# Value bias added on VectorE in the values' bank, epsilon added to one column, and no bias row on TensorE: a fused transformer layer

## The reference

```
ln(x)  = (x - mean) / sqrt(var + 1e-5)
x  = x + attn(ln(x));   x = x + ffn(ln(x))
attn(x): n = ln(x)*w + b;  Q, K = elu(n @ qk_w + qk_b) + 1   (64 features)
         V = n @ v_w + v_b                                  (256 features)
         out_t = sum_{s<=t} (q_t.k_s) V_s / (sum_{s<=t} q_t.k_s + 1e-6)
         x = x + out @ o_w + o_b;  x = x + gelu((ln(x)*w + b) @ f1 + f1_b) @ f2 + f2_b
ffn(x):  h = gelu(x @ ternary(W_fc));  (ln(h)*w + b) @ ternary(W_proj)
```

## Time and profile before

| | us |
|---|---|
| median of 3 runs (467.3 to 470.79) | 467.65 |
| the profiled execution's own time | 467.8 |
| its span, in which all rows below lie | 465.8 |
| PE, DVE, ACT busy in the span | 448.6, 369.0, 322.3 |

### The profile page before, as it was taken

How to read it: one execution, slowest core, us unless ns; L and a number is a source line. 1 busy time by engine, 2 the same in 40 slices (tenths; PEclk the granted TensorE clock), 3 DMA queues, 4 the chain that set the end, 5 groups by cost and what they waited for, 6 DMA issues and landing times.

```text
span 465.8 us, 8944 instructions
## 1 busy us (share of the span) xinstructions
PE 448.6 (96%) x3012; PEld 408.1 (88%) x3012; DVE 369.0 (79%) x1184; ACT 322.3 (69%) x606; POOL 187.5 (40%) x188
## 2 busy tenths in 40 slices
PE   4988999999999999999999999999999999999996
PEld 4876898889989999889989899889998999889875
DVE  6978969875898779985898868986898768767675
ACT  4976856988368864988468874788459793775262
POOL 3967025510565042640545123740545323540433
PEclk9977999999999999999999999999999999999999
DMA  7241000000020002000020002000020000000001
GB/s 236 117 181 45 1 2 1 1 23 2 1 68 2 25 0 69 2 23 1 2 68 2 24 0 70 0 24 2 1 68 2 23 1 15 9 2 24 0 23 46
DMA packets 10044, 14.08 MB, mean 30 GB/s; under 512 B 784, under 2 KB 9104, under 8 KB 9488
## 3 DMA queue, kind: packets, MB, share of 16 engines
q1 hardware_dynamic: 10000, 13.52, 8.6%
HBM read 9.32 MB, written 4.19 MB: 29 GB/s over the span
## 4 chain that ended last, share of the span: by engine, by line
PE 69%; issue 13%; POOL 6%; DVE 2%; ACT 1%; POOLq 0%; DVEq 0%; ACTq 0%
PE bank_f L415 10%; PE bank_p L445 10%; PE bank_f L203 5%; PE bank_f L204 5%; PE bank_f L205 5%; PE bank_y L204 5%; PE bank_y L203 5%; PE bank_y L205 5%; PE bank_y L429 4%; PE bank_a L203 3%; PE bank_a L205 3%; PE bank_a L204 3%; PE bank_a L211 2%; PE bank_f L211 1%; POOL rs L1155 1%
## 5 line engine op out<-in xcount | busy, mean ns | idle before, releaser
L1155 POOL TENSOR_TENSOR rs<-ve,neg_half 128x2 f32<-128x2 f32 x48 | 33.7, 701 | 227.3 <-DVE ve L846 225.5
L204 PE MATMUL bank_y<-wf_lo,h_hi 128*128 128x256 f32 x240 | 67.1, 280 | 0.0
L203 PE MATMUL bank_y<-wf_hi,h_hi 128*128 128x256 f32 x240 | 67.1, 279 | 0.0
L205 PE MATMUL bank_y<-wf_hi,h_lo 128*128 128x256 f32 x240 | 67.0, 279 | 0.0
L445 PE MATMUL bank_p<-wpj_t,g_hi 128*128 128x256 f32 x256 | 64.0, 286 | 0.3 <-DVE y_yc L1048 0.3
L445 PE MATMUL bank_p<-wpj_t,g_lo 128*128 128x256 f32 x256 | 62.4, 280 | 0.0
L1039 DVE SCALAR_TENSOR_TENSOR g_lo<-bank_y,vec,g_hi 128x256 fp32r<-128x256 f32 x128 | 54.9, 477 | 9.4 <-ACT g_hi L687 9.2
L687 ACT ACTIVATE g_hi<-bank_y,vec 128x256 fp32r<-128x256 f32 x128 | 52.5, 475 | 10.2 <-PE bank_y L429 8.2
L650 ACT ACTIVATE bank_f<-bank_f,f_bias 128x512 f32<-128x512 f32 x64 | 42.3, 660 | 23.7 <-PE bank_f L205 23.2
L415 PE MATMUL bank_f<-wfc_t,z3T_hi 128*128 128x512 f32 x128 | 53.9, 421 | 1.4 <-DVE z3T_lo L907 1.4
L203 PE MATMUL bank_f<-z2T_hi,wf_hi 128*128 128x512 f32 x128 | 53.3, 416 | 1.2 <-DVE z2T_lo L907 1.2
(11 more groups left out here) (293 smaller groups left out, 1209.5 us busy)
## 6 DMA issues: line engine op xcount, KB each, us to landing
out<-y_yc SPq DMA_DIRECT2D x16, 256.0 KB, 2.2
x_even<-in_x SPq DMA_DIRECT2D x8, 256.0 KB, 3.0
x_odd<-in_x SPq DMA_DIRECT2D x8, 256.0 KB, 3.1
h<-in_f SPq DMA_DIRECT2D x1, 1024.0 KB, 7.9
y_yc<-in_f SPq DMA_DIRECT2D x1, 1024.0 KB, 9.9
h<-in_fc SPq DMA_DIRECT2D x1, 1024.0 KB, 4.9
h<-in_pj SPq DMA_DIRECT2D x1, 1024.0 KB, 4.8
z<-in_wv SPq DMA_DIRECT2D x1, 256.0 KB, 4.0
```

What stands on the lines that cost most here:

```text
L203: pe.matmul(ps, w[0], r[0], start=start, stop=False, skip_group_check=skip)
L204: pe.matmul(ps, w[0], r[1], start=False, stop=False, skip_group_check=skip)
L205: return pe.matmul(ps, w[1], r[0], start=False, stop=stop, skip_group_check=skip)
L1155: pool.tensor_tensor(rs[n][:, 2 * h:2 * h + 2], ve[n][:, 2 * h:2 * h + 2], neg_half[:, 0:2], ALU.pow).then_inc(s[f"ln{n + 1}_rs"], 1)
```

## The change

It drops the bias row: `ones_row`, `eps_row`, `eps_hi`, `eps_raw`, their memsets, `eps_split`, `eps_lo` and the matmul at the head of each attend. Instead DVE adds the bias to each pair of value tiles in its bank before ACT and DVE split it (`v_bias`, 16 in all; `v_hi` now waits for it), and adds epsilon to the denominator's column with an instruction of one element per partition before the reciprocal (32 in all). POOL's `n1o` adds o_b alone and waits for its load instead of for `bo_rows`. The lists of all four engines are written anew.

```
 def attend(g, t):
-    pe.matmul(b[:, 0:VW], ones_row[:], eps_row[:], start=True, stop=False)
     for j in range(t + 1):
-        mm = split3(b[:, 0:VW], w, [r[:, j, :] for r in v], False, j == t)
+        mm = split3(b[:, 0:VW], w, [r[:, j, :] for r in v], j == 0, j == t)
 def v_hi(g, h):
-    act.wait_ge(s["v_done"], 2 * g + h + 1)
+    act.wait_ge(s["v_biased"], 2 * g + h + 1)
 def bo_rows():
-    dve.tensor_scalar(eps_raw[:, 0:D], bank_q[0:33, 0:D], -ATTN_EPS, None, ALU.mult)
-    dve.tensor_tensor(bo_b[:], bank_q[:, 0:D], ob_b, ALU.add)
+    dve.tensor_copy(bvo_b[:], bank_q[:, 0:D]).then_inc(s["bo_ready"], 1)
+def v_bias(g, h):
+    dve.wait_ge(s["v_done"], 2 * g + h + 1)
+    if g == 0:
+        dve.wait_ge(s["bo_ready"], 1)
+    dve.tensor_tensor(by_k(v_bank(g, h)), by_k(v_bank(g, h)),
+                      bvo_b[:].unsqueeze(1).to_broadcast([P, 2, D]), ALU.add).then_inc(s["v_biased"], 1)
 def attn_out(g, t):
-    dve.reciprocal(rden[:, t:t + 1], b[:, D:D + 1]).then_inc(s["rden_ready"], 1)
+    dve.tensor_scalar(den[:, t:t + 1], b[:, D:D + 1], 1.0, ATTN_EPS, ALU.mult, ALU.add).then_inc(s["den_ready"], 1)
+    dve.wait_ge(s["den_ready"], 4 * g + t + 1)
+    dve.reciprocal(rden[:, t:t + 1], den[:, t:t + 1]).then_inc(s["rden_ready"], 1)
```

The new lists where the prediction goes through them. DVE:

```
 first(): ... ln1_stats(1, 1); bo_rows(); qk_lo(0)
+  ln1_shift(1, 0); v_bias(0, 0); ln1_shift(1, 1); v_bias(0, 1); af_mask(0); ae_mask(0); ad_mask(0)
+  v_lo(0, 0); af_lo(0); ae_lo(0); ad_lo(0); v_lo(0, 1); attn_out(0, 0); attn_out(0, 1)
 ...
+  y_sum(0, 0); ln3_stats(0, 0); v_bias(1, 0); y_sum(0, 1); ln3_shift(0, 0); ln3_stats(0, 1); v_lo(1, 0)
+  ln3_shift(0, 1); v_bias(1, 1); z3_lo(0, 0); attn_out(1, 0); v_lo(1, 1); ln2_stats(1, 0); z3_lo(0, 1)
 step(g), before:
-  y_sum(g, 0); ln3_stats(g, 0); v_lo(g + 1, 0); y_sum(g, 1); ln3_shift(g, 0); ln3_stats(g, 1); v_lo(g + 1, 1)
-  output(g - 1, 1); ln3_shift(g, 1); attn_out(g + 1, 0); ln2_stats(g + 1, 0); z3_lo(g, 0)
 step(g), after:
+  y_sum(g, 0); ln3_stats(g, 0); y_sum(g, 1); v_bias(g + 1, 0); ln3_shift(g, 0); ln3_stats(g, 1); v_bias(g + 1, 1)
+  v_lo(g + 1, 0); ln3_shift(g, 1); output(g - 1, 1); v_lo(g + 1, 1); attn_out(g + 1, 0); z3_lo(g, 0)
 last():
+  y_sum(6, 0); ln3_stats(6, 0); v_bias(7, 0); y_sum(6, 1); ln3_shift(6, 0); ln3_stats(6, 1); v_lo(7, 0)
 ...
-  g_lo(7, 1, 0); output(7, 0); g_lo(7, 1, 1)
+  g_lo(7, 1, 0); g_lo(7, 1, 1); output(7, 0)
```

PE:

```
 first():
-  v_mm(0, 0); v_mm(0, 1); scores(0); f1b()
-  attend(0, 0); attend(0, 1); attend(0, 2); tu(1, 0); attend(0, 3); tu(1, 1); tz2(0, 0); tz2(0, 1)
-  theta_sum(0); f1(0, 0); f1(0, 1); theta_sum(1); qk_mm(1); f1(0, 2); f1(0, 3); f2(0, 0)
+  v_mm(0, 0); v_mm(0, 1); scores(0)
+  attend(0, 0); attend(0, 1); attend(0, 2); attend(0, 3); f1b(); tz2(0, 0); tz2(0, 1); tu(1, 0)
+  tu(1, 1); theta_sum(0); f1(0, 0); f1(0, 1); qk_mm(1); f1(0, 2); f2(0, 0); theta_sum(1); f1(0, 3)
 ...
-  v_mm(1, 0); v_mm(1, 1); attend(1, 0); attend(1, 1); tz3(0, 0)
-  attend(1, 2); fc(0, 0, 0); tz3(0, 1); attend(1, 3); fc(0, 0, 1); fc(0, 1, 0); fc(0, 1, 1)
+  v_mm(1, 0); v_mm(1, 1); tz3(0, 0); attend(1, 0)
+  attend(1, 1); tz3(0, 1); fc(0, 0, 0); attend(1, 2); fc(0, 0, 1); fc(0, 1, 0); attend(1, 3)
 step(g):
-  f2(g, 7); v_mm(g + 1, 0); v_mm(g + 1, 1); proj(g - 1, 1, 1)
-  proj(g - 1, 1, 2); proj(g - 1, 1, 3); tz3(g, 0); attend(g + 1, 0); attend(g + 1, 1)
-  attend(g + 1, 2); tz3(g, 1); fc(g, 0, 0); attend(g + 1, 3); fc(g, 0, 1); fc(g, 1, 0); fc(g, 1, 1)
+  f2(g, 7); proj(g - 1, 1, 1); v_mm(g + 1, 0)
+  v_mm(g + 1, 1); proj(g - 1, 1, 2); proj(g - 1, 1, 3); attend(g + 1, 0); tz3(g, 0); attend(g + 1, 1)
+  tz3(g, 1); attend(g + 1, 2); fc(g, 0, 0); fc(g, 0, 1); fc(g, 1, 0); fc(g, 1, 1); tr(g, 0, 0)
 last():
+  v_mm(7, 0); proj(5, 1, 1); v_mm(7, 1); proj(5, 1, 2); tz3(6, 0); proj(5, 1, 3); attend(7, 0)
 ...
-  tr(7, 1, 2); proj(7, 1, 0); tr(7, 1, 3); proj(7, 1, 1)
+  tr(7, 1, 2); tr(7, 1, 3); proj(7, 1, 0); proj(7, 1, 1)
```

ACT and POOL in `first()`:

```
 ACT
-  abs_part(0); u_norm(1, 1); u_hi(1, 0); abs_part(1); u_hi(1, 1); wf2_hi(3); z2_norm(0, 0)
-  z2_norm(0, 1); z2_hi(0, 0); z2_hi(0, 1); abs_part(2); abs_part(3); gelu(0, 0); h_hi(0, 0)
+  z2_norm(0, 0); abs_part(0); abs_part(1); z2_norm(0, 1); z2_hi(0, 0)
+  z2_hi(0, 1); u_hi(1, 0); u_hi(1, 1); abs_part(2); gelu(0, 0); h_hi(0, 0); abs_part(3); gelu(0, 1)
 POOL
-  wf1_lo(0); wf1_lo(1); wf1_lo(2); ln1_rstd(1, 0); wf1_lo(3); n1o(0); ln1_rstd(1, 1)
+  wf1_lo(0); ln1_rstd(1, 0); wf1_lo(1); ln1_rstd(1, 1); wf1_lo(2); n1o(0); wf1_lo(3)
```

More of the change, by code:

```diff
@@ L94, in build @@
         ob_b, f2b_b = rows_b[:, 0, :], rows_b[:, 1, :]
-        bo_b = sb("bo_b", [P, D])
+        bvo_b = sb("bvo_b", [P, D])
+        den = sb("den", [P, T])
         pj_rows_b = sb("pj_rows_b", [P, 2, D])
         csum_b, cpj_b = pj_rows_b[:, 0, :], pj_rows_b[:, 1, :]
[L98 to L101, removed]
         x_two = [sb("x_even", [P, T, D]), sb("x_odd", [P, T, D])]
@@ L307, in scores @@
                 if g == 0:
-                    pe.wait_ge(s["rows_w"], 8)
+                    pe.wait_ge(s["rows_w"], 4)
                 def block_of(ps, j, q0, q1):
@@ L697, in first @@
-                gelu(0, 1); h_hi(0, 1); gelu(0, 2); h_hi(0, 2); gelu(0, 3); h_hi(0, 3); qk_exp(1); qk_hi(1)
-                gelu(0, 4); h_hi(0, 4); k_dup(1); gelu(0, 5); rows(); h_hi(0, 5); gelu(0, 6); ae_hi(1); h_hi(0, 6)
-                ad_hi(1); gelu(0, 7); h_hi(0, 7); af_hi(1); n1(1); v_hi(1, 0); v_hi(1, 1); z3_norm(0, 0)
-                spread_copy(); z3_hi(0, 0); z3_norm(0, 1); u_norm(2, 0); z3_hi(0, 1); gelu3(0, 0, 0); gelu3(0, 0, 1)
-                gelu3(0, 1, 0); z2_norm(1, 0); gelu3(0, 1, 1); g_hi(0, 0, 0); gelu3(0, 2, 0); g_hi(0, 0, 1)
@@ new lines, in first @@
+                z2_hi(0, 1); u_hi(1, 0); u_hi(1, 1); abs_part(2); gelu(0, 0); h_hi(0, 0); abs_part(3); gelu(0, 1)
+                h_hi(0, 1); gelu(0, 2); h_hi(0, 2); gelu(0, 3); h_hi(0, 3); gelu(0, 4); qk_exp(1); h_hi(0, 4)
+                qk_hi(1); gelu(0, 5); k_dup(1); rows(); gelu(0, 6); h_hi(0, 5); n1(1); h_hi(0, 6); ad_hi(1)
+                gelu(0, 7); h_hi(0, 7); af_hi(1); ae_hi(1); v_hi(1, 0); z3_norm(0, 0); spread_copy(); z3_hi(0, 0)
+                z3_norm(0, 1); v_hi(1, 1); z3_hi(0, 1); gelu3(0, 0, 0); gelu3(0, 0, 1); gelu3(0, 1, 0)
@@ L1063, in first @@
-                ae_mask(1); ad_mask(1); ln1_stats(2, 1); h_lo(0, 5); n1_ve(2); h_lo(0, 6); ae_lo(1); ln1_shift(2, 0)
-                ad_lo(1); h_lo(0, 7); af_lo(1); y_sum(0, 0); ln3_stats(0, 0); y_sum(0, 1); v_lo(1, 0)
-                ln3_shift(0, 0); ln3_stats(0, 1); v_lo(1, 1); ln3_shift(0, 1); z3_lo(0, 0); attn_out(1, 0)
-                attn_out(1, 1); ln2_stats(1, 0); attn_out(1, 2); z3_lo(0, 1); ln2_stats(1, 1); ln2_var(1, 0)
-                ln2_stats(1, 2); attn_out(1, 3); ln2_shift(1, 0); ln2_stats(1, 3); ln2_var(1, 1); ln4_stats(0, 0)
@@ new lines, in first @@
+                h_lo(0, 5); ln1_stats(2, 1); ad_mask(1); h_lo(0, 6); n1_ve(2); ad_lo(1); af_mask(1); h_lo(0, 7)
+                ae_mask(1); af_lo(1); ae_lo(1); y_sum(0, 0); ln3_stats(0, 0); v_bias(1, 0); y_sum(0, 1)
+                ln3_shift(0, 0); ln3_stats(0, 1); v_lo(1, 0); ln3_shift(0, 1); v_bias(1, 1); z3_lo(0, 0)
+                attn_out(1, 0); v_lo(1, 1); ln2_stats(1, 0); z3_lo(0, 1); attn_out(1, 1); ln2_stats(1, 1)
+                ln1_shift(2, 0); ln2_var(1, 0); attn_out(1, 2); ln2_shift(1, 0); attn_out(1, 3); n1_shift(2)
```

239 lines of the change are left out of this document (112 added, 127 removed).

## The result

The kernel before took 469.03 us in the median of 20 runs, the changed one 471.54 in 20: a ratio of 1.0046, with a 95% interval of 1.0029 to 1.0063. It is slower by 0.5%: 2.2 us by the ratio, 2.5 between the two medians. The forecast was 467.3 and its range 463.0 to 470.8, on a base of 467.65; as ratios that is 0.9993 and up to 1.0067. The profiled execution took 470.49 us against 467.8; its span is 468.8 against 465.8, 3.0 more. The 20 times of the kernel before stand in two clumps, ten up to 468.49 and ten from 469.58, with the median between them, so that 1.4 of the distance from 467.3 to 471.54 lies in the base; and the profiles of e4 and e6, of over 600 us, are not read (e8 and e10 have their edits again).

What follows compares the result with a forecast made beforehand. It took a full TensorE queue, matmul start to start, as the bound. Start -2.0, g = 0 +1.2, passes +0.6, g = 6 -0.3, tail +0.25 sum to -0.25 on 467.8; forecast 467.3 us, range 463.0 to 470.8.

Steps and rivals of the forecast that it cites:

- a pass costs 53.26 - 0.48 + 0.6: Each pass of step(g): four bias products saved, one wait added; +0.12 us a pass, +0.6 in five.
- The wait in each pass: PE waits for v_lo at attend(g+1, 0), behind a DVE chain of 5.96 us; 0.6 us in each of five passes.
- The place for g = 0: From y_sum(0, 0) to fc(0, 0, 1), where no proj fills the wait: 11.05 us against 9.84, +1.2.
- The start: Up to f1(0, 3): f1b moved behind the attends lets the work there come earlier; -2.0 us.
- Rival 2: At the start, f1b meets the low clock, 7 us instead of 3.5, and nothing is gained; 470 us, chance 0.1.
- Last and tail: From y_sum(6, 0) on: -0.3 for g = 6, where other work hides the wait, and +0.25 at the end.
- (1): In the passes, DVE keeps up and PE does not wait; -3.0, 463.7 us, chance 0.26.
- (5): On DVE, each operation starts only when the one before has ended; wait 1.7 a pass, 473 us, chance 0.02.
- (3): In the passes, DVE at 86% becomes the bound and more items turn late; 470 to 472.5 us, chance 0.12.
- (4): In the passes, PE already hides the bias product, so a pass without it is as long; chance none.
- What PE saves, it waits back: Whole kernel: the prediction's summary of its sum, -0.25 us against the profiled 467.8.

Runs made afterwards that it cites:

- e4: Changed kernel with 64 unused bytes per partition ahead of x and tz3(g, 0) ahead of attend(g+1, 0), no fills; ratio 0.9992 to the kernel before.
- e6: Changed kernel with 64 unused bytes ahead of x and f1b put back ahead of the attends; ratio 1.0120 to the kernel before.
- e8: Changed kernel, 64 bytes ahead of x, tz3(g, 0) ahead of attend(g+1, 0), unread products ahead of tz3(0, 0) and attend(0, 0); ratio 0.9965 to before.
- e10: The kernel of e6 run again: changed, 64 unused bytes ahead of x, f1b ahead of the attends; ratio 1.0099 to the kernel before.
- e1: Changed kernel with 64 unused bytes per partition ahead of x, nothing else different; ratio 1.0009 to the kernel before.
- e7: Changed kernel with 64 unused bytes ahead of x and the value bias (v_bias) left out; ratio 0.9928 to the kernel before.
- e5: Changed kernel with 64 unused bytes ahead of x and 14 unread products on TensorE ahead of tz3(0, 0); ratio 0.9981 to the kernel before.
- e9: Changed kernel, 64 unused bytes ahead of h, v_lo(g+1, 0) ahead of v_bias(g+1, 1) on VectorE, 14 unread products ahead of tz3(0, 0); ratio 0.9983 to before.

## Why the prediction was wrong, by its steps

- **The step that failed** is the one that prices the pass: "a pass costs 53.26 - 0.48 + 0.6". It keeps the distance of every product that stays, and puts the effect of the dropped tiles at nothing. I had written that a pass costs the distance from one matmul's start to the next, and then treated that distance as fixed, though the change drops tiles and so moves those it is measured on. Place is worth 0.31 of the 0.46 by which a pass grew (e1: 53.42 against 53.74), 1.6 in five, 0.1 in the step from 0 to 1, and 0.2 from y_sum(6, 0) on: 1.9 us of the 3.25 missed between the two profiles. With 0.7 to 1.0 for the clock (below), some 0.5 is left over, in pieces of at most 0.2. Of the 4.2 us between 467.3 and 471.54 another 1.4 is the base, whose median of three runs lay in its lower clump, and 0.1 is a slip: 467.8 - 0.25 - 0.15 is 467.4.
- **The wait in each pass**: right. 5.96 for the chain, 0.61 for its cost, five times. With the old places the pass is +0.15 against +0.12 forecast, and here luck has a part. By e7 and e1 the two terms were -0.31 and +0.46, not -0.48 and +0.6: each was too large by some 0.15, and the errors cancel.
- **The place for g = 0**: the walk was right, the clock was not in it. Without the fall the step is 52.97 (e5) and 52.98 (e10), +1.18 against the forecast's +1.2. The fall adds 0.7 to 1.0; the forecast had no term for it.
- **The start**: 66.96 is -1.92 against -2.0; attend(0, 0) came at 23.39 (23.9 forecast), f1(0, 0) at 37.27 (36.2), gelu(0, 0) at 40.81 behind the table load (40.9). Rival 2 held in part: from 31 to 37 us PEclk is 0.50, and f1b with its follower takes 28.86 to 33.53, 4.67 instead of 3.5; the attends, done at 28.86 instead of 29.9, made it good. The rival's ground, that idle stretches stood ahead of the low clocks in rows 8, holds for one of the two: ahead of the first (22.6 to 29.5) TensorE had no gap of over 0.15 us from 18 us on, and what it ran last were f1b's one-column products. The hit itself is in part luck. Over all profiles read, y_sum(0, 0) lies at 66.8 to 69.3 with the changed lists (nine with v_bias and f1b behind the attends, mean 67.9) and at 68.6 to 69.9 with those of before (four, mean 69.0), so that the term is nearer to -1.1 than to -2.0.
- **Last and tail**: -0.05 forecast, +0.35 measured, +0.14 with the old places (e1).
- **The rivals**: (1) and (5) fall with the chain of 5.96. (3) gave the right time, 470 to 472.5, by the wrong mechanism: its sign was a pass of 54 or more with waits at tr, tu or f1; the pass is 53.74, and the view of waits has nothing in the passes but v_lo. (4) falls with e7, where the pass is shorter. The time of (3) was near enough to mislead; only the distances inside a full queue show the difference.

With the old places and the fill (e5) the changed kernel stands at 0.9981 (0.9957 to 1.0006), and the forecast was 467.3 / 467.65 = 0.9993. "What PE saves, it waits back" is what is left of it, with a start that gains less than forecast.

## What to carry to other kernels

When a change adds or drops a tile, list which later tiles move, and compare the distance of the matmuls in a full queue over a whole block, before any story about waits: here 64 bytes were worth as much as the edit itself. An idle stretch of TensorE can have a price behind it as well as in it, so a forecast that adds a wait of 1.9 us should carry a lower-clock case for what follows. And ask, when a wait is moved, which queue holds the next item: in e9 it was ScalarE's, behind an instruction that waits for the moved one.
